# Experts' results joined into words by VectorE in the expert stage, and input halves ahead of low parts

## The reference

```python
# x: 625 x 1024 float32, 10000 edges src -> dst, all widths 1024
x = x + gnn(layernorm(x), edges, W, b)      # linear, then normalised sum over neighbours
h = layernorm(x) @ lin0_w + lin0_b
h = silu(h @ w1 + b1) * (h @ w2 + b2)
# mixture of experts: 8 experts, the best 4 of each token, weights renormalised
routed = sum over the 4 chosen e of weight[e] * ((silu(h @ exp_w1[e]) * (h @ exp_w3[e])) @ exp_w2[e])
shared = (silu(h @ sh_w1) * (h @ sh_w3)) @ sh_w2        # hidden width 2048
h = (routed + shared) @ lin1_w + lin1_b
x = x + silu(h @ w1' + b1') * (h @ w2' + b2')
```

## Time and profile before

| | |
|---|---|
| median of three runs | 1546.89 us |
| profiled execution, its own time | 1547.93 us |
| its span | 1546.3 us |
| TensorE matmul busy | 1517.0 us, 98% |
| VectorE busy | 838.5 us, 54% |
| ScalarE busy | 649.8 us, 42% |
| GpSimd busy | 115.0 us, 7% |
| mean granted TensorE clock | 0.996 |
| moved by DMA | 230.04 MB, mean 149 GB/s |

### The profile page before, as it was taken

How to read it: one execution, slowest core, us unless ns; L and a number is a source line. 1 busy time by engine, 2 the same in 40 slices (tenths; PEclk the granted TensorE clock), 3 DMA queues, 4 the chain that set the end, 5 groups by cost and what they waited for, 6 DMA issues and landing times.

```text
span 1546.3 us, 27037 instructions
## 1 busy us (share of the span) xinstructions
PE 1517.0 (98%) x10412; PEld 1498.4 (97%) x10412; DVE 838.5 (54%) x1396; ACT 649.8 (42%) x934; POOL 115.0 (7%) x139
## 2 busy tenths in 40 slices
PE   9999999999999999999999999999999799999998
PEld 8998999999999999999999999999999799999998
DVE  8664569854533345454545455555553256345886
ACT  6322335542222344454444445454444475223442
POOL 1321010000100000001010100000000330001000
PEclk9999999999999999999999999999999899999999
DMA  4412212233522568888797878888768664221333
GB/s 138 135 42 68 68 42 86 94 111 120 143 83 82 147 182 214 218 190 238 191 241 197 239 205 226 213 208 251 190 189 203 183 183 121 91 69 56 102 113 84
DMA packets 168029, 230.04 MB, mean 149 GB/s; under 512 B 110580, under 2 KB 119330, under 8 KB 167914
## 3 DMA queue, kind: packets, MB, share of 16 engines
q1 hardware_dynamic: 142044, 182.07, 43.8%
q0 software_dynamic: 14976, 33.08, 7.2%
q10 hardware_dynamic: 10894, 13.26, 2.7%
HBM read 185.28 MB, written 18.95 MB: 132 GB/s over the span
## 4 chain that ended last, share of the span: by engine, by line
PE 84%; DVE 6%; ACT 4%; issue 3%; DMA 2%; ACTq 1%; POOL 0%; DVEq 0%; POOLq 0%
PE acc L1886 79%; PE acc L1866 3%; ACT w_hi L553 1%; DMA act_x<-y_dram,top_idx 1%; DVE yrow L1708 1%; ACT work L1013 1%; ACT gath L1056 1%; DVE w_lo L1357 1%; DVE work L1652 1%; ACT yrow L1056 1%; PE acc L1935 0%; DVE w_lo L1306 0%; DVE yrow L1122 0%; DMA y_dram<-yrow 0%; DVE yrow L1121 0%
## 5 line engine op out<-in xcount | busy, mean ns | idle before, releaser
L1886 PE MATMUL acc<-act_x,w_hi 128*128 128x312 f32 (+8 forms) x2304 | 509.1, 310 | 4.6 <-ACT act_x L985 3.9
L1886 PE MATMUL acc<-act_b,w_hi 128*128 128x312 f32 (+8 forms) x2048 | 449.7, 309 | 0.0
L1886 PE MATMUL acc<-act_a,w_hi 128*128 128x314 f32 (+1 forms) x1920 | 424.8, 311 | 14.8 <-ACT work L848 12.1
L1306 DVE TENSOR_TENSOR w_lo<-raw,w_hi 128x1024 fp32r<-128x1024 f32 x253 | 309.1, 1222 | 209.8 <-ACT w_hi L553 203.7
L1886 PEld LDWEIGHTS acc<-act_x,w_hi 128*128 128x128 f32 x2304 | 386.4, 189 | 7.2 <-issue 6.2
L1886 PE MATMUL acc<-act_x,w_lo 128*128 128x312 f32 (+8 forms) x1152 | 356.4, 309 | 0.0
L1886 PEld LDWEIGHTS acc<-act_b,w_hi 128*128 128x128 f32 x2048 | 342.2, 189 | 0.1
L1886 PEld LDWEIGHTS acc<-act_a,w_hi 128*128 128x128 f32 x1920 | 321.2, 191 | 17.2 <-ACT work L848 13.1
L1886 PE MATMUL acc<-act_b,w_lo 128*128 128x314 f32 (+8 forms) x1024 | 315.5, 308 | 0.0
L1886 PE MATMUL acc<-act_a,w_lo 128*128 128x314 f32 (+1 forms) x960 | 295.8, 308 | 0.0
L553 ACT ACTIVATE w_hi<-raw 128x1024 fp32r<-128x1024 f32 x264 | 276.9, 1050 | 5.6 <-PE acc L1886 4.6
(11 more groups left out here) (230 smaller groups left out, 1119.2 us busy)
## 6 DMA issues: line engine op xcount, KB each, us to landing
raw<-stream_dram SPq DMA_DIRECT2D x296, 512.0 KB, 3.9
y_dram<-yrow POOLq DMA_DIRECT2D x16, 512.0 KB, 6.0
y_dram<-yrow POOLq DMA_DIRECT2D x8, 352.0 KB, 7.3
rows<-x_dram ACTq DMA_DIRECT2D x1, 2500.0 KB
x_dram<-rows ACTq DMA_DIRECT2D x5, 500.0 KB
h_rows_dram<-rows ACTq DMA_DIRECT2D x1, 2500.0 KB
rows<-x_dram ACTq DMA_DIRECT2D x8, 312.5 KB
rows<-x_dram SPq DMA_DIRECT2D x5, 448.0 KB
```

Of the source, the lines that this page charges most:

```text
L1306: dve.tensor_tensor(w_lo[:, s, :], raw[:, s, :], w_hi[:, s, :].bitcast(f32), ALU.subtract).then_inc(lo_split, count)
L1886: ins = pe.matmul(o, w, xs_[h], start=(first and w is hi and xs_ is x_hi), stop=(last and w is lo))
```

## The change

Halves of the experts' results are joined into words in the expert stage. `y_rows(e)` on VectorE copies each of the three turned tiles of expert e from `yrow` into words in `gath`; it stands in expert e+1 at m = 1 of the up stage, ahead of the product, and for the last expert behind its down stage. GpSimd saves each tile of words when its copy is done, and `y_dram` holds float32 rows. The gather for the sum goes straight to the slots that `add_back` reads, and `back_rows` on ScalarE is gone; a gather into a slot waits for `add_back` to have read it. `add_back` and the transposes of the sum stand one pair later.

`x_stage` has three slots. The three gathers of an expert's input follow each other at once, ahead of the saves, and the turns stand behind the loads 14, 16 and 18. The first of them also waits for the saves out of `gath`. In the down stage VectorE's order for m is now: word m, low part of the weight, low part of chunk m.

```diff
-X_TURNS = (11, 15, 19)
+X_TURNS = (14, 16, 18)
-    y_dram = nc.dram_tensor("y_dram", (EXPERTS * CAP, 2 * D), u16).ap()
+    y_dram = nc.dram_tensor("y_dram", (EXPERTS * CAP, D), f32).ap()
-        x_stage = flat_b[:, 9 * D:10 * D].bitcast(u16)
+        x_stage = flat_b[:, 2 * KC * CAP:2 * KC * CAP + 3 * D].bitcast(u16).rearrange("p (n d) -> p n d", n=3)
...
+                if e >= 2 and n == 0:                            # turn_inputs
+                    sp.wait_ge(y_saved, 16 * 3 * (e - 1))
...
                 if e >= 1 and m == 0:                            # turn_outputs
-                    sp.wait_ge(y_saved, 16 * 3 * e)
+                    sp.wait_ge(y_words, 3 * e)
...
-                        turn_inputs(r + 1, n, x_stage, 3 * (r + 1) + n + 1)
+                        turn_inputs(r + 1, n, x_stage[:, n, :], 3 * (r + 2))
...
             def save_y(e):
-                for s in range(2):
-                    pool.wait_ge(y_turned[s], e * (8 * KC) + 8 * KC)
-                pool.sem_inc(save_go, 1)
                 for n, (c0, cn) in enumerate(SLOT_TILES):
+                    pool.wait_ge(y_words, e * 3 + (n + 1))
+                    pool.sem_inc(pool_go, 1)
                     pool.dma_start(y_dram[bass.ds(e * CAP + c0, cn), :],
-                                   y_halves[0:cn, :, n, :]).then_inc(y_saved, 16)
+                                   grow[0:cn, n, :]).then_inc(y_saved, 16)
...
                 gather_list(e + 1)
-                gather_tile(x_stage, 0)
+                for n in range(3):
+                    gather_tile(x_stage[:, n, :], n)
                 save_y(e - 1)
-                gather_rest(e + 1)
...
-                        pool.wait_ge(back_words, TOP * (i - 1) + k + 1)
-                    pool.indirect_dma_start(out=back_parts[0:TT, k, :, :].rearrange("p t d -> p (t d)"), out_offset=None,
-                                            in_=y_dram,
+                        pool.wait_ge(back_used, TOP * (i - 1) + k + 1)
+                    pool.indirect_dma_start(out=back_slot(k), out_offset=None, in_=y_dram,
...
-            def back_rows(i):                                    # ScalarE
-                for k in range(TOP):
-                    act.wait_ge(back[k], 16 * (i + 1))
-                    if i >= 1:
-                        act.wait_ge(back_used, TOP * (i - 1) + k + 1)
-                    act.activation(back_slot(k).bitcast(u16).rearrange("p (d t) -> p t d", t=2),
-                                   back_parts[0:TT, k, :, :], ACT.Copy).then_inc(back_words, 1)
...
+            def y_rows(e):                                       # VectorE
+                for s in range(2):
+                    dve.wait_ge(y_turned[s], e * (8 * KC) + 8 * KC)
+                for n, (c0, cn) in enumerate(SLOT_TILES):
+                    dve.tensor_copy(grow[0:cn, n, :].bitcast(u16).rearrange("p (d t) -> p t d", t=2),
+                                    y_halves[0:cn, :, n, :]).then_inc(y_words, 1)
...
                     weight_low(base, 2 * m + 3)
+                    if prev and m == 1:
+                        dve.wait_ge(x32_ready, e * KC + KC)
+                        y_rows(e - 1)
...
                 for m in range(KC):
-                    weight_low(base, UNITS_UP + m + 3)
                     if nxt:
                         if m == 0:
                             dve.wait_ge(unit_done, base + UNITS_UP)
-                        expert_in(e + 1, m)
-                if nxt:
-                    expert_in_lo(e + 1, KC - 1)
+                        expert_in_word(e + 1, m)
+                    weight_low(base, UNITS_UP + m + 3)
+                    if nxt:
+                        expert_in_lo(e + 1, m)
...
             expert(EXPERTS - 1, False)
+            dve.wait_ge(y_saved, 16 * 3 * (EXPERTS - 1))
+            y_rows(EXPERTS - 1)
...
                 gated_pair(shb, m, b_hi, b_lo, None)
-                if 2 <= m < NT + 2:
-                    add_tile(m - 2)
-                if 1 <= m <= NT:
-                    add_back(m - 1)
+                if 3 <= m < NT + 3:
+                    add_tile(m - 3)
+                if 2 <= m < NT + 2:
+                    add_back(m - 2)
```

More of the change, by code:

```diff
@@ L370, in build @@
         now_ready = sem("now_ready")
-        gather_go = sem("gather_go")
-        save_go = sem("save_go")
+        pool_go = sem("pool_go")
         xe_turned = sem("xe_turned")
@@ L378, in build @@
         y_turned = [sem(f"y_turned{s}") for s in range(2)]
+        y_words = sem("y_words")
         y_saved = sem("y_saved")
         back = [sem(f"back{s}") for s in range(TOP)]
-        back_words = sem("back_words")
         back_used = sem("back_used")
@@ L412, in build @@
         ov_tok_copied = sem("ov_tok_copied")
-        ov_go = sem("ov_go")
         ov_gathered = sem("ov_gathered")
@@ L628, in gather_tile @@
                                         ).then_inc(gathered, 16)
[L630 to L634, removed]
             pool.wait_ge(routed, 1)
@@ L675, in _ @@
                         pool.wait_ge(ov_tok_copied, n + 1)
-                        pool.sem_inc(ov_go, 1)
+                        pool.sem_inc(pool_go, 1)
                         pool.indirect_dma_start(out=ov_in.bitcast(u16), out_offset=None, in_=h_rows_dram,
@@ L1658, in expert_in_lo @@
                                   ALU.subtract).then_inc(xe_lo, 1)
[L1660 to L1663, removed]
             for m in range(KC):
+                expert_in_word(0, m)
                 weight_low(U_SHA, UNITS_UP + m + 3)
-                expert_in(0, m)
-            expert_in_lo(0, KC - 1)
+                expert_in_lo(0, m)
+            def y_rows(e):
[4 more added lines that the diff above has]
+                                    y_halves[0:cn, :, n, :]).then_inc(y_words, 1)
             def expert(e, nxt, prev=True):
@@ L1673, in expert @@
                     weight_low(base, 2 * m + 3)
+                    if prev and m == 1:
+                        dve.wait_ge(x32_ready, e * KC + KC)
+                        y_rows(e - 1)
                     dve.wait_ge(unit_done, base + (2 * m + 2))
                     dve.wait_ge(exp.silu, e * KC + (m + 1))
-                    if prev and m < 2:
-                        dve.wait_ge(y_turned[m], e * (8 * KC))
+                    if prev and m == 0:
+                        dve.wait_ge(y_turned[0], e * (8 * KC))
                     dve.tensor_tensor(e_prod[:, m % 2, 0:CAP], acc[:, (2 * m + 1) % 4, 0:CAP], e_silu,
@@ L1696, in _ @@
             expert(EXPERTS - 1, False)
+            dve.wait_ge(y_saved, 16 * 3 * (EXPERTS - 1))
+            y_rows(EXPERTS - 1)
             def add_back(i):
                 for k in range(TOP):
-                    dve.wait_ge(back_words, TOP * i + k + 1)
+                    dve.wait_ge(back[k], 16 * (i + 1))
                     w = top_w[0:TT, k, i:i + 1]
@@ L1795, in _ @@
                 chain[:] = main_chain
-            for s in range(2):
-                dve.wait_ge(y_turned[s], EXPERTS * (8 * KC))
             for m in range(KC):
                 gated_pair(shb, m, b_hi, b_lo, None)
+                if 3 <= m < NT + 3:
+                    add_tile(m - 3)
                 if 2 <= m < NT + 2:
-                    add_tile(m - 2)
-                if 1 <= m <= NT:
-                    add_back(m - 1)
+                    add_back(m - 2)
             for m in range(KC):
@@ L2279, in shb_extra @@
             def shb_extra(m):
-                if 2 <= m < NT + 2:
-                    i = m - 2
+                if 3 <= m < NT + 3:
+                    i = m - 3
                     pe.wait_ge(back_used, TOP * (i + 1))
```

6 lines of the change are left out of this document (removed).

## The result

The changed kernel takes 1523.41 us (median of four runs, 1522.4 to 1525.0) against 1546.36 for the kernel before in the same comparison. The ratio is 0.9853, 95% interval 0.9836 to 0.987. The forecast was 1523.5 within 1520.5 to 1532.

What follows compares the result with a forecast made beforehand. TensorE, busy 98% of the span, was taken as the bound, so gains come only from its waits and lower clock. 15.9 + 7.5 = 23.4 us off the median of 1546.89 gives 1523.5, range 1520.5 to 1532.

Steps and rivals of the forecast that it cites:

- Part 1: Removing back_rows from ScalarE shortens place A from 131.5 to 115.6 us: gain 15.9 us, of which the clock is 2.7.
- place A: Up stage of the shared expert's second half, 131.5 us before, where TensorE waits for ScalarE, once for 9.1 us.
- one ring: In place A, add_back, 10 us of ScalarE, SiLU and product follow each other, longer than TensorE's pair of units.
- Part 2: Sum's gathers and add_back in place A: 6 us of room at add_back(0), 3.3 us for later gathers; no cost taken.
- Part 3: y_rows on VectorE in the up stage: 1.33 us a copy, 4.0 us an expert, 32 us in all, no cost.
- The limit on its end: y_rows must end by 18.5 us (20.2 - 1.7) into the expert, or TensorE waits for weight 6.
- part 5: An expert's three input gathers go out together early, sharing DMA engines with the last output turns; effect: nothing.
- Part 4: GpSimd's saves follow the copies, landing 6.5 us later, at 21; SyncE's wait for them has 6 us of room: nothing.
- The Trainium skill's rule: VectorE copies using both ports keep GpSimd from writing DMA descriptors; saves start up to 4 us later, sum the same.
- Part 6: Down stage order word, weight's low part, input's low part: late starts of experts go, gain 7.5 us.
- The ring: Down stage: ScalarE and VectorE hand work round in 3.84 us, against TensorE's unit of 3.38 or 3.29 us.
- The rival with the other sign: y_rows becomes the up stage's late part; eats over 23.4 us from 3.8 us a copy; 1571 at 5 us; chance 0.03.

Runs made afterwards that it cites:

- rows_later: Kernel before with back_rows, add_back, the transposes of the sum and add_tile one pair later, ScalarE still joining: 1534.72 us, ratio 0.9932.
- copies_thrice: Changed kernel with each copy of y_rows made three times, each waiting for the one before: 1562.13 us, ratio 1.0099.
- gathers_late: Changed kernel with an expert's three input gathers held until all output turns of the expert before have landed: 1522.45 us, ratio 0.9856.
- turns_old: Changed kernel with the input turns behind loads 11, 15 and 19 as before: 1522.94 us, ratio 0.9857.
- saves_held: Changed kernel with all three saves of an expert waiting for its last copy: 1522.3 us, ratio 0.9854.
- short_rows: Kernel before with back_rows cut to 16 words of each 1024 and add_back reading other float32 data: 1538.9 us, ratio 0.9946.
- old_order: Changed kernel with the old order of the down stage: 1528.83 us, ratio 0.9893.

## Why the prediction was right, step by step

- **Part 1, place A.** 115.6 us forecast, 115.7 measured. The clean length, built from undisturbed units of the same stage, was the right way to price it: it took in the clock. The cause was given as one ring. It was two things: at tile 0 ScalarE's queue standing at a gather (9.1 us and 2.7 at the lower clock, cured by rows_later), and the ring in later tiles (about 4 us in the kernel before, 5.1 once tile 0 is cured, and taken away here by moving the join). The prediction named both waits but not their shares.
- **Part 2, the sum's gathers.** The cover held, but the room was overstated. "Lands 9.9 us later" was the old median; in the changed kernel the median is 11.7, and slot 3 comes late by up to 3.0 us. The last add_back ends at 1297.5 and TensorE asks at 1300.5: 3 us of the 6 are left. The step passed over that GpSimd's issue of a gather, 1.2 us at best, now takes up to 2.2 (over 2.1 in six of twenty). No run tests why, but the trace shows a pattern. Eleven of the twenty are issued while VectorE is inside an add of gathered rows (L1694), a low part (L1285) or a subtraction of the product (L1304), each with two tensors as input. All eleven end 1.06 to 1.17 us after that instruction does; the other nine take 1.19 to 1.22 us. Two of them, each below the instruction of VectorE that they meet (timelines of VectorE and GpSimd):

```profile
1231.01 2.67 DVE L1694 SCALAR_TENSOR_TENSOR yrow<-gath,top_w,yrow 125x1024 f32<-125x1024 f32 x2
1231.19 2.16 POOL L693 DMA_INDIRECT gath<-y_dram,top_idx  x1 [23.12 <-DVE yrow L1691]
1234.99 1.22 DVE L1285 TENSOR_TENSOR w_lo<-raw,w_hi 128x1024 fp32r<-128x1024 f32 x1
1235.16 2.12 POOL L693 DMA_INDIRECT gath<-y_dram,top_idx  x1 [0.30 <-DVE yrow L1694]
```

The change brings this about itself: a slot is now freed by VectorE's own read, so the gather into it is often issued just behind the start of VectorE's next add.
- **Part 3, y_rows.** 1.33 us forecast, 1.34 measured, and no cost. The limit on its end, 6 units less 1.7 us, held in the test: 27 us of waits forecast for copies_thrice, 25.9 measured. Its start was off. "9.5 at worst against 10.3" became a start at 13.4 us in expert 5, since part 5's early gathers slow the output turns, which part 5 counted as nothing by taking the longest turn of the old trace. gathers_late shows it. It cost room, not time.
- **Part 4, saves.** Saves landed in 4.5 us (median), not 6.5, and SyncE never waited for them. The wait on SyncE was covered even at load 11, as turns_old shows.
- **The Trainium skill's rule** in SBUF — State Buffer (section "SBUF: two separate sides") was weighed and left the sum alone. Its effect is there: the first save of each group takes up to 1.99 us beside the copies and at most 0.59 without them. This trace and saves_held agree with it, for the saves; the price is off TensorE's way.
- **Part 6, the order.** 7.5 us forecast; 7.9 measured alone and 6.2 by its removal, both within their intervals. By the stages it is 7.9 us: 4.1 in expert 7, 1.6 in expert 6 and 1.2 in expert 5, where 4.1, 1.5 and 1.1 were reckoned, and 1.0 in experts 3 and 4 for the 0.8 that was an estimate by trend. The ring was right, but not its lag. The prediction set 3.84 us against units of width 304 and 296, yet the input of expert 5, 6 or 7 is made in the down stage of the expert before, at 316, 312 and 304, where TensorE's unit takes 3.50, 3.45 and 3.35 us in the trace. The lag is 0.34 to 0.49 us a unit, not 0.45 to 0.55; the gain didn't rest on it, as it was read from the starts of the experts.
- **The rival with the other sign.** Its mechanism is real, but its price was too low: it counted the waits and left out the lower clock behind most of them. In copies_thrice the seven waits of 2.5 to 5.4 us cost 25.9 us, and the lower clock behind six of them 1.5 to 3.0 us each, half as much again in all. The change turns to a loss nearer than the stated 3.8 us a copy: at three times 1.34 us, 4.0 a tile, it is already 15 us slower than the kernel before by the ratio, where the prediction's own working (7 x 3.8 us of excess, less 23.4) gives 3.

The sum met the median to 0.1 us, and that is luck: the runs of one kernel spread over 2.6 us, and against the kernel before in the same comparison the gain was 22.95 us, not 23.4. The terms themselves are good. By the stages place A gave 15.8 us for 15.9, and the experts 7.9 for 7.5.

## What to carry to other kernels

Ask of a wait whether the engine works or stands in its queue: a join that waits for a gather ahead of urgent work costs its place, and moving it one turn down the same list gave nearly half of the gain here (10.5 of 22.7 us by the ratios) without taking any work away. Price a stage by its own undisturbed units, which counts the clock too, and check a planned cover by doubling and tripling the work under it. Where two engines hand work to each other every turn, compare the round of that ring with the bound's turn, not the busy shares: 3.84 us against 3.35 to 3.50, at 54% and 42% busy. And compare stages as well as totals: at the same clock they repeat to 0.2 us here, where the totals of one kernel spread by up to 7 us.

## What the runs showed of the hardware

- A wait of about 2 us before TensorE's matmuls was followed by the lower clock in some executions and not in others: behind the same wait of 2.0 to 2.1 us at the start of expert 7 the kernel before and short_rows ran at 1.2 GHz for a stretch and lost about 1.5 us, old_order and rows_later lost none. In copies_thrice it followed a wait of 2.5 us, and didn't follow one of 3.0.
- ScalarE's copy of 2048 16-bit elements to every other element takes 2.53 us on 125 partitions; VectorE's takes 1.34 on 128 and 1.33 on 88.
- A save issued by GpSimd beside VectorE's three copies in a row ends 0.12 to 0.13 us behind the last of them, up to 1.99 us after its start; alone it takes 0.53 to 0.59. A gather of the sum issued in the changed kernel while VectorE was inside an instruction with two tensors as input ended 1.06 to 1.17 us behind that instruction; the others took 1.19 to 1.22 us. Three in the kernel before, issued 0.05 to 0.06 us behind such an instruction's start, weren't held and took 1.20.
- Beside the gathers of the input, a DMA transpose on another queue lands up to 12.4 us after its issue, 6.0 without them.
